# Layer norm from sums of squares, two load slots and grouped transposes in a fused attention and feed-forward kernel

## What is computed

```python
def _layernorm(x, axis=-1, eps=1e-5):
    m = jnp.mean(x, axis=axis, keepdims=True)
    v = jnp.var(x, axis=axis, keepdims=True)
    return (x - m) / jnp.sqrt(v + eps)

def attn(X, Wq, Wk, Wv):
    Q, K, V = X @ Wq, X @ Wk, X @ Wv
    s = jnp.where(causal, Q @ K^T, -inf)
    return softmax(s / sqrt(64)) @ V

def qat_lora_linear(x, W, b, A, B):
    scale = max(|W|) / 127
    Wq = clip(round(W / scale), -128, 127) * scale
    return x @ Wq^T + b + 2.0 * (x @ A^T) @ B^T

x = x + attn(_layernorm(x))
x = x + ffn(_layernorm(x))    # linear(1024->4096), gelu, linear(4096->1024)
```

## Time and profile before

| | us |
|---|---|
| median of the runs shown (2 runs, 7413.9 to 7673.27) | 7543.58 |
| the profiled execution, its own time | 7401.95 |
| its span on the slowest core (core 2) | 7400.4 |
| spans of the eight cores | 7375.5 to 7400.4 |
| TensorE busy, matmuls | 6213.9 (84%) |
| VectorE busy | 1113.7 (15%) |
| ACT busy | 468.0 (6%) |

### The profile page before, as it was taken

The page is one execution under the profiler, slowest core; times in us unless marked ns, Lnnn a source line. Parts: engine busy times, 40 slices in busy tenths (PEclk is TensorE's granted clock), DMA queues, the critical chain, the costliest instruction groups (busy, mean ns, idle before and its releaser), DMA issues.

```text
span 7400.4 us, 47028 instructions; the slowest of 8 cores (7375.5 to 7400.4 us)
## 1 busy us (share of the span) xinstructions
PE 6213.9 (84%) x14779; PEld 2825.5 (38%) x14779; DVE 1113.7 (15%) x2587; ACT 468.0 (6%) x1186; POOL 159.5 (2%) x276
## 2 busy tenths in 40 slices
PE   5666666666767777778789999999999999999998
PEld 2333332333322333333334444444444444444443
DVE  3322123211133232322220000000000000000000
ACT  0001000011000000000001111111110000000000
POOL 0000000000000000000000000000000000000000
PEclk8765667655677888888779999999999999999999
DMA  4322223322211000000121111111116656566565
GB/s 127 96 75 73 64 86 109 94 75 78 88 60 43 26 28 24 26 17 18 43 80 54 46 43 57 43 43 57 43 53 206 206 197 207 197 206 206 191 207 174
DMA packets 238864, 696.69 MB, mean 94 GB/s; under 512 B 36529, under 2 KB 102353, under 8 KB 230434
## 3 DMA queue, kind: packets, MB, share of 16 engines
q1 hardware_dynamic: 134786, 290.14, 12.3%
q10 hardware_dynamic: 64672, 202.21, 8.7%
q0 software_dynamic: 39168, 201.34, 6.7%
HBM read 509.04 MB, written 184.55 MB: 94 GB/s over the span
## 4 chain that ended last, share of the span: by engine, by line
PE 79%; DVE 8%; DMA 6%; issue 4%; ACT 2%; DVEq 0%; ACTq 0%; SPq 0%; POOLq 0%; POOL 0%
PE ps L212 76%; PE ps L217 3%; ACT A L502 2%; DMA A<-wpr 1%; DMA A<-wfc 1%; DMA xa<-A 1%; DMA A<-w2t 1%; DVE A L484 1%; DVE stats L281 1%; DVE stats L492 1%; DVE A L324 1%; DVE A L327 1%; DVE A L540 1%; DVE A L321 1%; DMA AW<-hT 0%
## 5 line engine op out<-in xcount | busy, mean ns | idle before, releaser
L212 PE MATMUL ps<-A 128*128 128x512 f32 (+1 forms) x7232 | 3210.1, 591 | 135.1 <-DVE A L520 133.8
L212 PEld LDWEIGHTS ps<-A 128*128 128x128 f32 (+1 forms) x7232 | 1419.1, 210 | 1680.7 <-issue 1675.8
L212 PE MATMUL ps<-A,AW 128*128 128x512 f32 x4096 | 1776.1, 596 | 60.7 <-DMA A<-w2t 26.3
L212 PEld LDWEIGHTS ps<-A,AW 128*128 128x128 f32 x4096 | 780.0, 191 | 1056.7 <-issue 1056.7
L217 PE MATMUL ps<-identt,A 128*128 128x128 f32 (+2 forms) x1105 | 362.3, 356 | 561.2 <-DVE A L369 228.9
L658 DVE TENSOR_TENSOR A<-ps,A 128x512 f32<-128x512 f32 x64 | 44.1, 689 | 3457.4 <-PE ps L212 3454.2
L212 PE MATMUL ps<-AW,A 128*128 128x512 f32 x1024 | 505.3, 657 | 0.0
L217 PEld LDWEIGHTS ps<-identt,A 128*128 128x128 f32 (+2 forms) x1105 | 170.2, 161 | 840.5 <-issue 833.2
L212 PE MATMUL ps<-identt,A 128*128 128x128 f32 x512 | 234.7, 458 | 290.2 <-DVE A L327 290.2
L212 PEld LDWEIGHTS ps<-AW,A 128*128 128x128 f32 x1024 | 218.6, 217 | 267.7 <-issue 267.7
L606 ACT ACTIVATE AW<-ps,sbfc 128x512 f32<-128x512 f32 x256 | 176.1, 688 | 1695.2 <-PE ps L212 1300.0
(11 more groups left out here) (63 smaller groups left out, 1166.2 us busy)
## 6 DMA issues: line engine op xcount, KB each, us to landing
A<-w2t SPq DMA_DIRECT2D x256, 512.0 KB, 5.3
A<-w2t ACTq DMA_DIRECT2D x256, 512.0 KB, 4.6
hT<-AW POOLq DMA_DIRECT2D x32, 2048.0 KB, 7.6
AW<-hT SPq DMA_DIRECT2D x512, 128.0 KB, 3.5
A<-wfc ACTq DMA_DIRECT2D x64, 512.0 KB, 5.3
A<-x SPq DMA_DIRECT2D x64, 512.0 KB, 3.3
xa<-A POOLq DMA_DIRECT2D x64, 512.0 KB, 4.4
A<-wpr ACTq DMA_DIRECT2D x64, 512.0 KB, 5.8
```

Source lines behind the costliest of these rows:

```text
L212: e.matmul(_o, _l, _r, start=_st, stop=_sp, is_transpose=_tr),
```

## The change

1. **Layer norm.** `emit_ln_bn` goes. In its place the sum of the tile is taken on VectorE (one reduction of 1024) and the sum of squares on ACT (two Square activations of 512 with an accumulator, whose output goes to PSUM bank 7, or 6 in attention). Four operations of single columns on VectorE make the variance; then in stage one ACT takes Sqrt and VectorE the reciprocal, in attention ACT takes Ln and Exp as before; VectorE forms minus mean times inverse root, and ACT normalises the whole 128x1024 tile with one Identity activation.
2. **Weight slots.** Raw units land in two slots, `pL[u % 2]`, where there were three.
3. **Grouped transposes.** In `pv_phase` four blocks are transposed into one PSUM bank and copied by one 128x512 copy to one half of A7, which is now 1024 wide. Two groups (up to eight blocks) are transposed ahead of the first product; group g+2 stands behind the last product of group g.

```diff
@@
-    A7 = sb("A7", [128, 512])
+    A7 = sb("A7", [128, 1024])
@@
-    pL = [A2[:, 0:1024], A2[:, 1024:2048], A2[:, 5248:6272]]
-    bpL = [Buf("pL0"), Buf("pL1"), Buf("pL2")]
+    pL = [A2[:, 0:1024], A2[:, 1024:2048]]
+    bpL = [Buf("pL0"), Buf("pL1")]
@@
-                sl = pL[u % 3]
+                sl = pL[u % 2]
...
@@
-    def emit_ln_bn(xslot, bslot, cb, bstat):
-        vop(lambda e, s, _x=xslot: e.bn_stats(ST[:, cb:cb + 6], _x[:, 0:512]),
-            [bslot], [bstat])
-        vop(lambda e, s, _x=xslot: e.bn_stats(ST[:, cb + 6:cb + 12],
-                                              _x[:, 512:1024]),
-            [bslot], [bstat])
-        vop(lambda e, s: e.bn_aggr(ST[:, cb + 12:cb + 14], ST[:, cb:cb + 12]),
-            [bstat], [bstat])
...
     def emit_ln(xslot, bslot):
-        emit_ln_bn(xslot, bslot, 40, bLN1)
+        vop(lambda e, s, _x=xslot: e.reduce_sum(stc(c_sum), _x, AX.X),
+            [bslot], [bST[c_sum]])
+        sop(lambda e, s, _x=xslot: e.activation(psum[7][:, 0:512], _x[:, 0:512],
+                                                AF.Square, accum_out=stc(c_sq)),
+            [bslot], [bPS[7], bST[c_sq]])
+        sop(lambda e, s, _x=xslot: e.activation(psum[7][:, 0:512], _x[:, 512:1024],
+                                                AF.Square, accum_out=stc(c_tm)),
+            [bslot], [bPS[7], bST[c_tm]])
+        vop(lambda e, s: e.tensor_add(stc(c_sq), stc(c_sq), stc(c_tm)),
+            [bST[c_sq], bST[c_tm]], [bST[c_sq]])
+        vop(lambda e, s: e.tensor_scalar_mul(stc(c_m), stc(c_sum), 1.0 / D),
+            [bST[c_sum]], [bST[c_m]])
+        vop(lambda e, s: e.tensor_mul(stc(c_tmp), stc(c_m), stc(c_m)),
+            [bST[c_m]], [bST[c_tmp]])
+        vop(lambda e, s: e.scalar_tensor_tensor(
+            stc(c_var), stc(c_sq), 1.0 / D, stc(c_tmp), ALU.mult, ALU.subtract),
+            [bST[c_sq], bST[c_tmp]], [bST[c_var]])
+        sop(lambda e, s: e.activation(stc(c_tm), stc(c_var), AF.Sqrt,
+                                      bias=stc(c_eps)),
+            [bST[c_var], bST[c_eps]], [bST[c_tm]])
+        vop(lambda e, s: e.reciprocal(stc(c_r), stc(c_tm)),
+            [bST[c_tm]], [bST[c_r]])
+        vop(lambda e, s: e.scalar_tensor_tensor(
+            stc(c_nmr), stc(c_m), -1.0, stc(c_r), ALU.mult, ALU.mult),
+            [bST[c_m], bST[c_r]], [bST[c_nmr]])
+        sop(lambda e, s, _x=xslot: e.activation(_x, _x, AF.Identity,
+                                                bias=stc(c_nmr), scale=stc(c_r)),
+            [bST[c_nmr], bST[c_r], bslot], [bslot])
@@
     def emit_ln2p(xslot, bslot):
-        emit_ln_bn(xslot, bslot, 24, bLN2)
...
+        sop(lambda e, s: e.activation(stc(d_t1), stc(d_var), AF.Ln,
+                                      bias=stc(c_eps)),
+            [bST[d_var], bST[c_eps]], [bST[d_t1]])
+        sop(lambda e, s: e.activation(stc(d_r), stc(d_t1), AF.Exp,
+                                      scale=np.float32(-0.5)),
+            [bST[d_t1]], [bST[d_r]])
...
@@
-        def ptrans(kc):
-            tb = 2 + (kc % 2)
-            tr(psum[tb][:, 0:128], Pbuf[:, 128 * kc:128 * kc + 128], ident[:],
-               [bA2s[kc // 4], bident], [bPS[tb]])
-            vop(lambda e, s, _kc=kc, _tb=tb: e.tensor_copy(
-                A7[:, 128 * (_kc % 4):128 * (_kc % 4) + 128], psum[_tb][:, 0:128]),
-                [bPS[tb]], [bA7[kc % 4]])
-
-        ptrans(0)
-        if i >= 1:
-            ptrans(1)
+        def pgroup(g):
+            tb = 2 + (g % 2)
+            n = min(4, i + 1 - 4 * g)
+            for j in range(n):
+                kc = 4 * g + j
+                tr(psum[tb][:, 128 * j:128 * j + 128],
+                   Pbuf[:, 128 * kc:128 * kc + 128], ident[:],
+                   [bA2s[kc // 4], bident], [bPS[tb]])
+            vop(lambda e, s, _g=g, _tb=tb, _n=n: e.tensor_copy(
+                A7[:, 512 * (_g % 2):512 * (_g % 2) + 128 * _n],
+                psum[_tb][:, 0:128 * _n]),
+                [bPS[tb]], [bA7[4 * (g % 2) + j] for j in range(n)])
+
+        ngrp = (i + 4) // 4
+        pgroup(0)
+        if ngrp > 1:
+            pgroup(1)
         for kc in range(i + 1):
...
-            if kc + 2 <= i:
-                ptrans(kc + 2)
+            if kc % 4 == 3 and g + 2 < ngrp:
+                pgroup(g + 2)
```

More of the change, by code:

```diff
@@ L163, in build_program @@
     sones = sb("sones", [1, 128])
-    ST = sb("stats", [128, 56])
+    ST = sb("stats", [128, 32])
     c_sum, c_sq, c_m, c_var, c_r, c_nmr = 0, 1, 2, 3, 4, 5
@@ L191, in build_program @@
     bA5 = [Buf("A5_0"), Buf("A5_1")]
-    bA7 = [Buf(f"A7_{i}") for i in range(4)]
+    bA7 = [Buf(f"A7_{i}") for i in range(8)]
     bPS = [Buf(f"ps{i}") for i in range(8)]
@@ L197, in build_program @@
     bsones = Buf("sones")
-    bST = [Buf(f"st{i}") for i in range(56)]
+    bST = [Buf(f"st{i}") for i in range(32)]
     bHBM = {k: Buf(k) for k in ("xa", "hT", "w1t", "w2t", "y")}
@@ L278, in gen_prep @@
                         stc(c_wmax), _sl, AX.X, ALU.max, apply_absolute_value=True),
-                        [bpL[u % 3]], [bST[c_wmax]])
+                        [bpL[u % 2]], [bST[c_wmax]])
                 else:
@@ L458, in emit_ln2p @@
     def emit_ln2p(xslot, bslot):
-        emit_ln_bn(xslot, bslot, 24, bLN2)
+        vop(lambda e, s, _x=xslot: e.reduce_sum(stc(d_sum), _x, AX.X),
+            [bslot], [bST[d_sum]])
+        sop(lambda e, s, _x=xslot: e.activation(psum[6][:, 0:512], _x[:, 0:512],
+                                                AF.Square, accum_out=stc(d_sq)),
+            [bslot], [bPS[6], bST[d_sq]])
+        sop(lambda e, s, _x=xslot: e.activation(psum[6][:, 0:512], _x[:, 512:1024],
+                                                AF.Square, accum_out=stc(d_t1)),
+            [bslot], [bPS[6], bST[d_t1]])
+        vop(lambda e, s: e.tensor_add(stc(d_sq), stc(d_sq), stc(d_t1)),
+            [bST[d_sq], bST[d_t1]], [bST[d_sq]])
+        vop(lambda e, s: e.tensor_scalar_mul(stc(d_m), stc(d_sum), 1.0 / D),
+            [bST[d_sum]], [bST[d_m]])
+        vop(lambda e, s: e.tensor_mul(stc(d_t2), stc(d_m), stc(d_m)),
+            [bST[d_m]], [bST[d_t2]])
+        vop(lambda e, s: e.scalar_tensor_tensor(
+            stc(d_var), stc(d_sq), 1.0 / D, stc(d_t2), ALU.mult, ALU.subtract),
+            [bST[d_sq], bST[d_t2]], [bST[d_var]])
+        sop(lambda e, s: e.activation(stc(d_t1), stc(d_var), AF.Ln,
[4 more added lines that the diff above has]
+            [bST[d_t1]], [bST[d_r]])
+        vop(lambda e, s: e.scalar_tensor_tensor(
+            stc(d_nmr), stc(d_m), -1.0, stc(d_r), ALU.mult, ALU.mult),
+            [bST[d_m], bST[d_r]], [bST[d_nmr]])
+        sop(lambda e, s, _x=xslot: e.activation(_x, _x, AF.Identity,
+                                                bias=stc(d_nmr), scale=stc(d_r)),
+            [bST[d_nmr], bST[d_r], bslot], [bslot])
     def s_phase(i):
```

21 lines of the change are left out of this document (11 added, 10 removed).

## The result

The median over all 12 runs of the changed kernel is 8286.04 us, against 8072.81 us over the 11 runs of the kernel before. Over the other executions the changed kernel is slower by 0.8%: the ratio is 1.008, with a 95% interval of 1.0041 to 1.0118. That is a small loss that the 2% bound calls "same". The profiled execution took 7465.77 us, against 7401.95.

What follows compares the result with a forecast made beforehand. A serial chain through VectorE and ACT between TensorE's products was taken to bound stage one and attention. Terms +56 + 23 + 38 + 1 - 15 + 12 - 18 = +97 on 7401.95 gave 7499 us, range 7435 to 7610.

Steps and rivals of the forecast that it cites:

- third load late: Stage one, maximum pass: with two slots the third weight load delays the third reduction 2.8 us in 20 tiles, +56 us.
- norm in stage one: Stage one: longer serial chain, 23 us in 21 tiles beside the maximum pass, 38 us in 11 beside the quantising pass.
- norm in attention: Attention: normalisation waiting for the store moves to ACT, VectorE free 0.5 us earlier in 31 tiles, -15 us.
- grouped transposes: Attention: first product 0.40 us later in 29 tiles, +12 us; 129 fewer transposes among products, -18 us.
- table load: One more load of ACT's function table, for Sqrt in stage one ahead of attention's functions: 1.3 us.
- two rivals: The slow ones: late load at burst price, 7565 us, 15%; ACT table reloads in every tile, 7581 us, 3%.
- Single loads of this size land in 4.5 us: Stage one, maximum pass: landing time assumed for the third weight load, making the third reduction 2.8 us late.
- costs what a burst does: Rival, stage one: late load takes 7.8 us as loads issued together do, 122 us instead of 56, 7565 us; 15%.
- 336 remain: 129 fewer: Attention: transposes left among products, from 465, once the first eight of each tile stand ahead; saving 18 us.
- ACT loaded its table once more and not per tile: Rival: functions not fitting one set cost two loads in each of one stage's 32 tiles, 82 us more, 7581 us; 3%.
- The eight early transposes did not raise the clock: Rival, attention: transposes ahead of the products raise TensorE's clock sooner, gaining 70 us, 7429 us; 6%.
- Hidden load: Rival, stage one's maximum pass: the late load hides, its 56 us go and the rest stays, 7443 us; 12%.

Runs made afterwards that it cites:

- two slot experiments: Kernel before with two raw-weight slots instead of three: stage one 2031.1 us, +42.6; with one slot: stage one 2135.8 us, +147.3.
- reordered version: Three slots, old stage-one norm, grouped transposes, attention normalisation on ACT; stage one's norm and transposes moved ahead of weight preparation: stage one 1932.6 us against 1979.1 unmoved.

## Where the prediction was right, and the step that failed

It said 7499 us, +97 on the profiled execution; measured +64 there and +62 on the mean of the cores. Place and sign of every term held, and so did the mechanisms: the late third load, the longer chain, the store's wait that leaves VectorE's queue. The sum is half as large again as what was measured. The step that failed is the range, and with it two readings that sized terms wrongly; they follow behind the table. Term by term, with what measured it:

| term | predicted | measured | by |
|---|---|---|---|
| third load late | +56 | +43 | slots alone |
| norm in stage one | +61 | +53 | norm alone |
| norm in attention | -15 | -26 | norm alone |
| grouped transposes | -6 | -6 | groups alone |
| table load | +1 | one of 1283 ns more | not taken alone |

**The range.** 7435 to 7610 holds the executions that this document compares (7463.01 to 7493.08), but not the median over all runs, 8286.04. The step that failed is the reading of "the two runs shown are 259 us apart". The prediction meant its number "for runs like" the lower one, made the range from the ends of the sum and two rivals alone, and so put the difference between executions of one kernel at nothing, although 259 us is 2.7 times the effect that it forecast. What the runs showed in its place: 7401.93 to 8364.29 us for the kernel before and 7463.01 to 8441.62 for the changed one, a spread of over 900 us in each. A range widened by the 259 us would still have missed the median; two runs could not show the whole spread. That the forecast agrees with the compared executions rests on that choice.

**The slots.** "Single loads of this size land in 4.5 us" is the term that was mis-sized most: +56, measured +43. That median is of loads in the quantising pass; they are issued right behind a small LoRA load on the same queue. In the place where it counts a single load lands in 3.5 us beside the pass over W_fc, under the lower bound of 3.8, and in 4.2 beside the pass over W_proj. The lateness is 2.1 us a tile over the 20 tiles, where 2.8 was forecast. The lesson is to ask in which company a median was taken. Whether the small load makes the difference was not tested. The rival "costs what a burst does" needed about 7 us and falls.

**The norm in stage one.** The chains came out as worked out: 4.47 us beside the maximum pass (4.57 expected), and TensorE's wait 5.2 us beside the quantising pass (5.3 expected). The Identity took 1240 ns (1.24 expected). But there is luck in the second chain. I took the nearest row, 0.81 us, for a square. It measured 0.60. The price of the Trainium skill (ScalarE: Activation LUTs, What ACT_TABLE_LOAD costs) for immediate scale and bias, 186 ns + 0.833 ns a column, gives 0.61 as an estimate, and the trace agrees. That would make the term smaller, yet from the end of the evacuation (626.08) to the first small step (627.97) it is 1.89 us, where the prediction has 1.7. Two squares of 0.60 and two reads of the accumulator of 0.19 fill only the time to 627.50, and the hand-over to VectorE takes the other 0.47. The square was priced too high, and the reads and the hand-over too low.

The exponential reads scale and bias from columns of their own, the square has them as constants. The Ln of one column shows what this costs, with a constant bias before and one from a column now:

```profile
L361 ACT ACTIVATE stats<-stats 128x1 f32<-128x1 f32 x64 | 12.9, 202 | 1728.8 <-DVE stats L359 1728.8
```

```profile
L479 ACT ACTIVATE stats<-stats 128x1 f32<-128x1 f32 x32 | 9.4, 295 | 34.9 <-DVE stats L476 34.9
```

That is 0.09 us for one such operand; two would make up the 0.2 us between a square and an exponential.

**Attention.** That the store's wait would leave VectorE's queue was right, and the gain was larger than forecast: 3.38 us to the next scores where 3.7 were expected, -26 us where -15 were. About half of the missing 0.3 us is in the squares (1.63 us to the first small step, 2777.53 to 2779.16, where 1.8 was expected), the rest in the small steps and hand-overs behind them.

**The grouped transposes.** The -6 agrees with the forecast partly by luck. "336 remain: 129 fewer" is miscounted: with the first eight of each tile ahead, 1 + 2 + ... + 24 = 300 remain, 165 fewer. At the prediction's own prices (0.11 us, a third of them at twice that) the saving is then 24 us instead of 18, and with the +12 of the later first product, which the trace shows (0.40 us), the term would be -12. Measured is -6.4.

**The other rivals.** ACT loaded its table once more and not per tile: three loads of 1283 ns, where the kernel before has two. The eight early transposes did not raise the clock. "Hidden load" fell with the two slot experiments.

## What to carry to other kernels

Where two engines hand a tile back and forth, count the serial chain between two stretches of TensorE work, not the busy shares: here ACT was 6% busy, and moving the normalisation to it lost about 30 us in one stage (it stood at the end of the chain) and gained 47.5 in another (there it took a wait for a store off the engine that was needed next). An in-place pass over a tile that is being stored was best given to the engine that nobody waited for. A prefetch slot fewer cost the landing of the load less what it could hide behind, in each round in which the ring was too short, and twice as many waits cost 3.5 times as much when the cover was gone. When an agreement is checked, check the terms too: two of them here came out right by errors that cancel.

## What was unexpected of the hardware

A 128x512 Square with an accumulator and immediate operands took 0.60 us on ACT, an exponential over the same shape with operands read from SBUF 0.81. Back-to-back transposes in mid-stream cost 0.11 us each, no more than single ones between products. A 512 KB load issued alone landed in 3.3 us on the median beside the maximum pass of W_fc and in 4.2 beside that of W_proj, in the kernel with one slot; the loads of x, of the same size, did so too (3.3 and 4.3). No run here says why. In the reordered version TensorE waited 4.6 us less ahead of a tile's transposes beside a maximum pass, and the tile became 4.3 us shorter, since its value products took some 0.4 us longer.
